# A transformer step on one core: GELU cut into two scaled fp16 parts, wider FFN ranges, and the last stage in one listed order

## What is computed

```python
def _L0_ffn_ref(x, w1, b1, w2, b2):
    w1q = _bit_quant(w1)          # -1, 0 or 1
    w2q = _bit_quant(w2)
    h = jnp.einsum('bsd,fd->bsf', x, w1q) + b1
    h = jax.nn.gelu(h, approximate=False)
    return jnp.einsum('bsf,df->bsd', h, w2q) + b2

x = x + _L0_attn_a_ref(_layernorm(x), ...)   # 16 heads of 16, softmax over 1024 keys
x = x + _L0_ffn_ref(_layernorm(x), L0_ffn_w1, L0_ffn_b1, L0_ffn_w2, L0_ffn_b2)
x = x + _L0_attn_b_ref(_layernorm(x), ...)   # softmax over the heads of each token
x = x + _L0_ffn_ref(_layernorm(x), L0_ffn_w1, L0_ffn_b1, L0_ffn_w2, L0_ffn_b2)
```

## Time and profile before

| | |
|---|---|
| time, median of 3 runs | 401.43 us (399.44 to 403.08) |
| time of the profiled execution | 400.46 us |
| its span, first to last instruction | 398.4 us |
| PE busy / DVE / ACT / POOL, share of the span | 91% / 77% / 62% / 38% |
| the tail, 196.5 to 398.4 us | 201.9 us |
| mean granted TensorE clock | 0.953 of full |

### The profile page before, as it was taken

How to read it: one execution, slowest core, us unless ns; L and a number is a source line. 1 busy time by engine, 2 the same in 40 slices (tenths; PEclk the granted TensorE clock), 3 DMA queues, 4 the chain that set the end, 5 groups by cost and what they waited for, 6 DMA issues and landing times.

```text
span 398.4 us, 6021 instructions
## 1 busy us (share of the span) xinstructions
PE 361.1 (91%) x2157; PEld 174.6 (44%) x2157; DVE 307.9 (77%) x501; ACT 248.7 (62%) x433; POOL 150.2 (38%) x169
## 2 busy tenths in 40 slices
PE   7998969999999999999999979987987898877696
PEld 3643422222222222222234438855764464555485
DVE  7459998999999999999713446867999868999643
ACT  2573227999999999999997572323640453562431
POOL 4060079990000000000000023358687758847243
PEclk9999997999999999999999999998999588996899
DMA  7867643535000000000000000000000000000001
GB/s 199 265 108 124 144 97 64 116 62 112 2 1 2 1 2 1 2 2 1 1 2 1 2 0 2 0 2 0 2 1 2 0 0 2 26 1 2 26 2 53
DMA packets 14672, 14.22 MB, mean 36 GB/s; under 512 B 5235, under 2 KB 12979, under 8 KB 14454
## 3 DMA queue, kind: packets, MB, share of 16 engines
q1 hardware_dynamic: 12214, 11.70, 13.0%
q10 hardware_dynamic: 2176, 1.64, 1.4%
q0 software_dynamic: 256, 0.52, 0.8%
HBM read 5.40 MB, written 1.06 MB: 16 GB/s over the span
## 4 chain that ended last, share of the span: by engine, by line
PE 67%; DVE 23%; ACT 6%; issue 3%; POOL 1%; ACTq 0%; POOLq 0%; DVEq 0%
PE ps L1354 16%; PE ps L1340 14%; PE ps L1317 7%; PE ps L1494 7%; DVE mx L1051 4%; DVE s_wide L1152 4%; PE ps L1269 4%; PE ps L1483 3%; DVE xn L980 3%; PE ps L1468 3%; DVE pack L1141 3%; DVE stats L963 2%; PE ps L1529 2%; PE ps L1258 2%; PE ps L1299 2%
## 5 line engine op out<-in xcount | busy, mean ns | idle before, releaser
L869 ACT ACTIVATE pbuf<-ps,exp_scale 128x512 f32<-128x512 f32 x256 | 156.4, 693 | 15.9 <-PE ps L1340 12.8
L1051 DVE TENSOR_REDUCE mx<-ps 128x1 f32<-128x1024 f32 x128 | 150.2, 1218 | 9.9 <-PE ps L1317 6.7
L1340 PE MATMUL ps<-pack 64*128 64x512 f16 x256 | 87.9, 386 | 2.1 <-ACT pbuf L869 1.4
L1354 PE MATMUL ps<-pbuf,v_slot 128*32 128x512 f32 x512 | 69.1, 611 | 2.2 <-ACT pbuf L869 1.1
L1340 PEld LDWEIGHTS ps<-pack 64*128 64x128 f16 x256 | 23.2, 94 | 87.3 <-ACT pbuf L869 63.8
L1494 PE MATMUL ps<-w_nat,pack 128*128 128x256 bf16 x384 | 53.6, 286 | 1.8 <-POOL pack L719 1.8
L731 POOL TENSOR_TENSOR pbuf<-wT 128x1024 f32<-128x1024 f32 (+3 forms) x32 | 49.9, 1573 | 11.1 <-ACT wT L920 11.1
L1317 PE MATMUL ps<-pack 64*128 64x512 f16 x128 | 48.9, 385 | 5.0 <-DVE mx L1051 4.7
L719 POOL TENSOR_TENSOR pack<-pack 128x256 bf16<-128x256 f32 x64 | 42.0, 667 | 24.8 <-DVE pack L1141 24.8
L1317 PE MATMUL ps<-parts,pack 64*128 64x512 f16 x128 | 49.9, 395 | 0.0
L1141 DVE TENSOR_TENSOR pack<-pack 128x256 f32<-128x256 f32 x64 | 35.1, 558 | 18.1 <-ACT pack L914 18.0
(11 more groups left out here) (136 smaller groups left out, 389.0 us busy)
## 6 DMA issues: line engine op xcount, KB each, us to landing
w_nat<-in_L_ffn_w_dram SPq DMA_DIRECT2D x2, 1024.0 KB, 6.9
pack<-pack SPq DMA_DIRECT2D x3, 512.0 KB, 4.9
pack<-pbuf SPq DMA_DIRECT2D x20, 64.0 KB, 2.7
x_res<-in_L_attn_a_x_dram SPq DMA_DIRECT2D x4, 256.0 KB, 3.8
...
```

What stands on the lines that cost most here:

```text
L869: act.activation(pbuf[:, c % 2, j, :], ps[:, b, :], ACT.Exp, scale=exp_scale[:, 0:1]).then_inc(drained[b], 1)
L1051: dve.tensor_reduce(mx[:, par, k:k + 1], ps[:, b:b + 2, :].rearrange("p b k -> p (b k)"), AX_X, ALU.max) \
L1340: pe.matmul(ps[:, b, :], k_group[0:ROWS, at, j, P * c:P * c + P].rearrange("p g t -> p (g t)"), q_rows[0:ROWS, at, qh, j, :].rearrange("p ...
L1354: ins = pe.matmul(ps[32 * j:32 * j + 32, PV_BANK, :], v_slot[:, qh, c, j, :], pbuf[:, c % 2, j, :], start=(c == 0), stop=(c == TT - 1))
```

## The change

Three things at once.

**GELU in two parts.** `gelu` now writes its result back into the same PSUM bank, in fp32. A new event `g_hi` (ScalarE) multiplies it by `g_unit`, a power of two for each feature that `find_gelu_unit` takes from b1, into fp16; `g_lo` (VectorE) computes the scaled value minus `g_hi`, also in fp16, and only this drains the bank. GpSimd's `g3` is gone. `add_hidden` does 2 matmuls for a tile in place of 3, with `g_hi` and `g_lo` (fp16) against `w2T` (still bf16), which now carries the inverse of the power of two.

**Ranges.** FFN 0 has two ranges of 4 tiles (512 tokens); FFN 1 has one of 4 tiles and two of 2. `h`, `gelu`, `g_hi`, `g_lo` then take 512 columns at once where the range has 4 tiles. Four ranges may be kept at once (`KEPT`), before three.

**Order.** The tables of planned times are gone. `TAIL_ORDER` lists the 524 events one by one (before there were 638).

```diff
-RANGES = (((0, 2), (2, 2), (4, 2), (6, 2)), ((0, 2), (2, 2), (4, 2), (6, 2)))
+RANGES = (((0, 4), (4, 4)), ((0, 4), (4, 2), (6, 2)))
-KEPT = 3
-RANGE = 256
+KEPT = 4
+RANGE = 512
...
+TAIL_ORDER = (
+    ('exp', 4), ('w', 0), ('exp', 5), ('score', 3), ('exp', 6), ('w', 1), ('score', 4), ('score', 5), ('exp', 7), ('score', 6),
...
-            def third_gelu_part(r, s, f):
-                k = kept(r, s)
-                pool.wait_ge(g_rest, number["h", r, s, f] + 1)
-                pool.tensor_tensor(g_low[:, k, f, :], g_left[:, k, f, :], g_mid[:, k, f, :, 1], ALU.subtract) \
-                    .then_inc(g3_ready, 1)
...
             def gelu(key):
                 _, r, s, f = key
-                src = is_filled(act, key)[:, 0:RANGE]
+                src = is_filled(act, key)[:, 0:P * RANGES[r][s][1]]
+                act.activation(src, src, ACT.Gelu, bias=b1_col[:, f:f + 1]).then_inc(gelu_ready, 1)
+
+            def gelu_hi(r, s, f):
...
+                act.wait_ge(gelu_ready, number["h", r, s, f] + 1)
+                width = P * RANGES[r][s][1]
+                act.mul(g_hi[:, kept(r, s), f, 0:width], bank(("h", r, s, f))[:, 0:width], g_unit[:, f:f + 1]) \
+                    .then_inc(g_hi_ready, 1)
...
-                    dve.tensor_copy(w2T[:, 4 * c:4 * c + 4, :].rearrange("p f d -> p (f d)"), src) \
+                    dve.tensor_tensor(w2T[:, 4 * c:4 * c + 4, :], src.rearrange("p (f d) -> p f d", f=4),
+                                      g_unit_back[:, 4 * c:4 * c + 4].unsqueeze(2).broadcast_to([P, 4, D]), ALU.mult) \
...
-            def gelu_rest(r, s, f):
-                k = kept(r, s)
-                is_drained(dve, ("h", r, s, f))
-                dve.tensor_tensor(g_left[:, k, f, :], g_full[:, k, f, :], g_top[:, k, f, :, 1], ALU.subtract).then_inc(g_rest, 1)
+            def gelu_lo(r, s, f):
+                key = ("h", r, s, f)
+                width = P * RANGES[r][s][1]
+                dve.wait_ge(g_hi_ready, number[key] + 1)
+                dve.scalar_tensor_tensor(out=g_lo[:, kept(r, s), f, 0:width], in0=bank(key)[:, 0:width],
+                                         scalar=g_unit[:, f:f + 1], in1=g_hi[:, kept(r, s), f, 0:width],
+                                         op0=ALU.mult, op1=ALU.subtract).then_inc(drain_sem(key), 1)
...
+            def find_gelu_unit():
+
+                dve.wait_ge(cols_in, 16)
+                link(dve.tensor_scalar(g_bits[:, :], b1_col[:, :].bitcast(U32), MAGNITUDE, None, ALU.bitwise_and))
...
+                dve.tensor_scalar(g_unit[:, :], g_bits[:, :].bitcast(F32), G_TOP, None, ALU.mult).then_inc(g_unit_ready, 1)
...
-                    for n, part in enumerate((g_top[:, k, f, v, 1], g_mid[:, k, f, v, 1], g_low[:, k, f, v])):
-                        ins = pe.matmul(out, part, w2T[:, f, :], start=False,
-                                        stop=(f == FC - 1 and n == NPART - 1 and i == 1))
+                    at = P * (2 * p + i - RANGES[r][range_of(r, 2 * p)][0])
+                    v = slice(at, at + P)
+                    for n, part in enumerate((g_hi, g_lo)):
+                        ins = pe.matmul(out, part[:, k, f, v], w2T[:, f, :], start=False,
+                                        stop=(f == FC - 1 and n == 1 and i == 1))
```

192 lines of the change are left out of this document (104 added, 88 removed).

## The result

The changed kernel takes 367.87 us (median of 4 runs, 367.65 to 368.07) against 401.65 us for the one before on the same chip (4 runs, 399.44 to 403.08): a ratio of 0.916 with a 95% interval of 0.912 to 0.921. The profiled execution has a span of 366.2 us, 32.2 us less than before, at a mean granted clock of 0.967 (before 0.953).

The account below looks back on a forecast made before the run. It took TensorE as bound at the tail's start and end, TensorE and VectorE jointly in the heads. Savings of 15.7 us (middle), 5.3 (end) and 1.0 (start) made 22.0 off a 398.4 span: 378 us forecast, range 359 to 392.

Parts of the forecast that it names:

- What bounds it, stretch by stretch: Tail behind 196.5 us: TensorE bounds its start and end; TensorE and VectorE lean on each other in the heads stretch.
- Products, 9.1 us booked: y products, 384 matmuls to 256 at 0.109 us: 13.9 us of work, 5.3 saved in the middle, 3.8 at the end.
- the rival at the fp32 price: y matmuls of fp16 against bf16 run at the fp32 price, 0.156 us more each: 418 us; chance 0.02.
- GELU's subtraction, 3.6: VectorE in the middle: 64 subtractions, 35.1 us, become 40 of 23.3 us; 3.6 us saved on the chain.
- contention, 2.9 + 1.5: Middle: without `g3`, VectorE and GpSimd hold each other up less; normalising saves 2.9 us, the small causal addition 1.5.
- ScalarE, 1.4 gained and 1.0 lost: Middle: four fewer table loads save 1.4 us, the longer way through a bank costs 1.0; idle time covers added work.
- Start, 1.0 booked: First stretch of the tail: wider `h` blocks ahead of the last `pv`; 1 us saved, between 4 saved and 3 lost.
- Ranges and order, 2.0 us in the middle: Heads stretch: the new list recovers some VectorE idle time and lost clock; 2 us, between nothing and 14.
- The cover at the end, 2.5: End: pair 2's hidden blocks and y products cover TensorE's wait for the last normalising; 2.5 us saved, 1.0 lost elsewhere.
- the order pays more: VectorE's idle time and the heads' half-clock stretches go beyond 14 us: below 362, down to 350; chance 0.12.
- the clock takes it back: With less y work TensorE idles more and its clock falls: 391, up to 400; chance 0.06 for 392 to 400.
- banks held too long: Banks wait for GELU, `g_hi` and `g_lo`, stopping TensorE in the six-bank ring at 8 tiles: 396 or 406; chance 0.05.

## Why the prediction was right, and where its sum was not

The forecast was 378 us, between 359 and 392, and faster at 0.90; it came to 367.9. The side and the range held. The sum had 22.0 us of span and it was 32.2, and it was put together wrongly in the middle: the arithmetic was booked at some 17 us and is worth 2 by itself, the ranges and the order at 2 in the middle and, on top of the arithmetic, are worth 26 there. That the total still fell into the range is in part luck.

- **What bounds it, stretch by stretch: right at the end, half right in the middle.** The end is TensorE's: 6.5 us gained, 5.3 booked. In the middle the chain's shares were read as time that can be taken out piece by piece. The two products in the old order took L1494 down from 11.5 to 3.3% of the chain, 11 us, and gained 1.1 us for the 5.3 booked.
- **Products, 9.1 us booked.** The price was right: 40 in 4.54 us, 0.11 each, fp16 parts against bf16 weights, so the rival at the fp32 price is out. In the new order they carry 11.5 us, in the old one 4.6.
- **GELU's subtraction, 3.6, and contention, 2.9 + 1.5.** `g_lo` takes 746 and 480 ns where 690 and 420 were booked; VectorE's busy time in the tail fell from 135.5 to 123.3 us. `g_lo` never waited: no record is above 753 ns, with GpSimd's load put back neither. Normalising fell from 776 to 619 ns (booked 590), but not by the mechanism booked. Without `g3` in the old order it stayed at 755, and with the load back in the new one it is 651. It fell because 20 of 24 now stand where no head product is under way, and the four that meet one take 1.0 to 2.4 us: right in size, by luck. The small addition did not fall at all: 692 ns. The 1.5 us for it failed outright. GpSimd's products, which stay, are what it meets: the four that begin beside one take 0.80 to 1.62 us, the other four 0.22. In the old order all this together is worth nothing in the middle: tile 7 leaves at 371.65.
- **ScalarE, 1.4 gained and 1.0 lost.** 8.3 us more in the tail (10 to 12 booked). GELU and `g_hi` together are busy 45.7 us against 28.9 before, 16.8 more where 17.0 were booked. (One takes 670 or 698 ns over 512 columns; the 615 booked is a time from start to start, and they overlap a little in a row.) It isn't a bound in the new order, but becomes one in the old one: 19.7 us of waits of VectorE for it there.
- **Start, 1.0 booked.** It brought nothing: the milestone came 0.5 us later.
- **Ranges and order, 2.0 us in the middle, from a range of 0 to 14.** This is the mis-sized term, and the place where the sum went wrong. With the new arithmetic held fixed the new order and ranges together are worth (0.9950 - 0.9163) x 401 = 31.6 us over the whole kernel, 26 of them in the middle, the arithmetic alone in the old order 2. The new list doesn't do it without the wide ranges: with ranges of 256 it takes 396.8 us. This split depends on what is changed first. Inside the new order the third product costs 11.5 us and GpSimd's load 8.1, so if these two add up, the new order with the old arithmetic would be worth some 14 us and not 31.6. That kernel was not run. Nor was an order made for the old arithmetic with wide ranges; part of the 11.5 and 8.1 may be that the list doesn't suit the heavier load. The argument that pairs leaving the FFN together would make the heads stretch thinner had the wrong sign. In the first 33.4 us of that stretch VectorE is now busy 31.5 us and TensorE 30.9, before 28.8 and 28.7; both pairs' heads run beside the second half of the FFN.
- **The cover at the end, 2.5.** The cover is there: TensorE is busy 16.93 of the last 16.96 us. (The 3.12 us that the prediction reads are the weight load's wait; the matmul's own is 2.84.) With the arithmetic held fixed the end goes from 23.0 to 20.2 us, 2.8 for the 2.5 - 1.0 booked. Joining the last two ranges costs 6 us: 3.2 of waits, some 1.7 of clock, the rest open.
- **Rival "the order pays more": in kind, not in size.** Its mechanism, idle time of VectorE and half-clock stretches filled, is what happened, but the time is not below its 362. VectorE is idle 9.3 us of the heads stretch (before 15.2), and the middle's clock went from 0.90 to 0.92.
- **Rival "the clock takes it back".** Not in the changed kernel, though half-clock stretches remain (0.55 on average from 318 to 326 us). In the old order the kernels without `g3` fell from 0.90 to 0.86 in the middle, which is at most 5.5 us of 137. That may take part of the gain there, not all: the one that kept `g3` had 0.91 and gained as little. The rule of the Trainium skill (TensorE: Matmul & The Clock Gate, "HAM oscillation") that gaps between bursts bring the low clock fits these two runs by direction. The third, with a third of the y products gone and the clock not lower, doesn't show it.
- **Rival "banks held too long": wrong in the changed kernel, right as a mechanism.** It priced the time that one bank is held. What counted was how many tokens a bank stands for: with 512 in each the ring isn't felt, with 256 the same list loses 23 us to it. The condition stood in the prediction's own numbers: a bank held 2.9 us and more, and 5.2 us of hidden blocks in the ring.

What stays open: what a tuned order for the old arithmetic would take, what the other 5.6 of the 13.5 us of "issue" are, and whether some order for 256-token ranges would come near 368 us. Only two orders were tried with them.
